# Attention scores on row halves, normalisation moved to the routing phase, value products of two steps together

## The reference

```python
x = L0_attn_x                       # (4, 2048, 256), float32
xn = _layernorm(x, axis=-1)
x = x + _L0_attn_ref(xn, ...) + _L0_ffn_ref(xn, ...)
# inside _L0_ffn_ref:
h = _rmsnorm(xn, g1)
q = (h @ Wq).reshape(B, S, 16, 16); c = h @ Wdkv
k = (c @ Wuk).reshape(B, S, 16, 16); v = (c @ Wuv).reshape(B, S, 16, 16)
scores = where(causal, einsum("bqhd,bkhd->bhqk", q, k) / sqrt(16), -1e9)
out = einsum("bhqk,bkhd->bqhd", softmax(scores, axis=-1), v).reshape(B, S, D)
x2 = xn + out @ Wo
x2 = x2 + _moe(_rmsnorm(x2, g2), gate_w, w1, w2)   # 8 experts, 2 per token
```

## Time and profile before

| | us |
|---|---|
| runs of the kernel before (3) | 3376.55, 3378.97, 3382.85; median 3378.97 |
| the profiled execution, its own time | 3397.75 |
| its span in the profile | 3396.2 |
| PE, DVE, ACT, POOL busy in it | 2743.9, 2474.5, 1561.3, 2210.9 |
| phase 1 / phase 2 / phase 3 | 0 to 467 / 467 to 2277 / 2285 to 2570 |

### The profile page before, as it was taken

One profiled execution on the slowest core, in us unless ns is written; L12 is line 12 of the kernel. 1 busy time (PEld: TensorE's weight loads), 2 busy tenths in 40 slices (PEclk: granted clock), 3 DMA queues, 4 the chain that ended last, 5 costly groups with the idle time before them and its releaser, 6 DMA issues. The chain is left out here.

```text
span 3396.2 us, 56592 instructions
## 1 busy us (share of the span) xinstructions
PE 2743.9 (81%) x16988; PEld 1397.0 (41%) x17168; DVE 2474.5 (73%) x3932; ACT 1561.3 (46%) x2346; POOL 2210.9 (65%) x1179
## 2 busy tenths in 40 slices
PE   5959978998989898989899989977766988889700
PEld 2535532333333323332333333226655777777600
DVE  5538868877878797889778887714444999999444
ACT  2312235565656665666556666662222444444200
POOL 3423359678767966796669777964663666666476
PEclk9979999999999999999999999997767999999855
DMA  4995560443144214422442240016546666666676
GB/s 135 215 287 194 190 151 18 62 62 54 31 63 64 45 39 63 64 41 44 62 62 36 47 64 14 19 33 222 193 143 214 215 210 199 210 201 206 216 219 208
DMA packets 366323, 408.79 MB, mean 120 GB/s; under 512 B 66690, under 2 KB 310788, under 8 KB 366084
## 3 DMA queue, kind: packets, MB, share of 16 engines
q1 hardware_dynamic: 320132, 323.96, 39.2%
q0 software_dynamic: 17920, 54.55, 5.0%
q10 hardware_dynamic: 28032, 27.27, 2.3%
HBM read 256.12 MB, written 149.03 MB: 119 GB/s over the span
## 5 line engine op out<-in xcount | busy, mean ns | idle before, releaser
L885 DVE TENSOR_REDUCE p_piece_max<-p_ring 128x1 f32<-128x512 f32 (+3 forms) x2160 | 1319.0, 656 | 189.1 <-PE p_ring L1010 94.5
L959 ACT ACTIVATE p_probs<-p_st 128x1024 f32<-128x1024 f32 (+3 forms) x1280 | 1078.0, 894 | 682.5 <-PE p_st L1045 342.4
L827 POOL TENSOR_TENSOR p_terms<-p_head_p,p_head_in 128x4096 f32<-128x4096 f32 x32 | 347.7, 10865 | 314.4 <-ACT p_head_p L966 313.7
L1042 PE MATMUL p_st<-unit_q,unit_k 98*128 98x512 bf16 (+7 forms) x1642 | 433.7, 353 | 51.5 <-DMA unit_q<-p_neg_lo 31.5
L1057 PE MATMUL p_pv<-p_probs,unit_vg 128*32 128x512 f32 (+3 forms) x3520 | 409.6, 542 | 0.0
L1687 POOL TENSOR_TENSOR p_pv<-p_pr,p_qkv 128x4096 f32<-128x4096 f32 x32 | 347.8, 10868 | 38.6 <-ACT p_pr L1785 37.9
L1004 PE MATMUL p_ring<-unit_k,unit_q 64*128 64x512 bf16 (+3 forms) x1600 | 275.2, 358 | 75.0 <-DVE p_piece_max L885 74.5
L1858 PE MATMUL p_y_ps<-p_w,p_hid 128*128 128x256 f32 x1152 | 281.0, 400 | 31.6 <-ACT p_hid L1798 31.6
L812 POOL TENSOR_TENSOR p_terms<-p_head_in 128x4096 f32<-128x4096 f32 x32 | 282.0, 8814 | 4.9 <-POOL p_head_s L820 4.4
L1845 PE MATMUL p_hid_ps<-p_rT,p_w 128*128 128x256 f32 x1152 | 263.9, 382 | 4.8 <-issue 4.3
L833 POOL TENSOR_TENSOR p_terms<-p_terms 128x2048 f32<-128x2048 f32 (+2 forms) x96 | 252.6, 2632 | 17.1 <-POOL p_terms L833 11.4
(11 more groups left out here) (202 smaller groups left out, 3825.4 us busy)
## 6 DMA issues: line engine op xcount, KB each, us to landing
p_w<-ffn_w SPq DMA_DIRECT2D x144, 512.0 KB, 5.2
qk_parts<-p_parts SPq DMA_DIRECT2D x64, 384.0 KB, 3.3
head_qkv<-p_heads SPq DMA_DIRECT2D x16, 1536.0 KB, 6.2
p_rows<-sorted_rows SPq DMA_DIRECT2D x72, 256.0 KB, 4.5
expert_rows<-p_y ACTq DMA_DIRECT2D x72, 256.0 KB, 5.8
unit_q<-qk_parts SPq DMA_DIRECT2D x132, 128.0 KB, 10.3
unit_k<-qk_parts SPq DMA_DIRECT2D x132, 128.0 KB, 10.8
p_x<-attn_x SPq DMA_DIRECT2D x32, 512.0 KB, 5.2
```

What stands on the lines that cost most here:

```text
L827: step(nc.gpsimd.tensor_tensor(terms[:, :, :, :], head_p[:, u, :, :].unsqueeze(2).to_broadcast([P, H, DH, H]), head_in[:, u, 2, :, :].rear ...
L885: nc.vector.tensor_reduce(piece_max[:, h:h + heads, i, pc], ring_ps[bank][:, 0:heads * width].rearrange("p (h k) -> p h k", h=heads), AX_X ...
L959: nc.scalar.activation(probs[:, 2 * turn_of(s, i) + u, :, 0:width], st_ps[u][:, :, 0:width], ACT.Exp).then_inc(probs_done, 1)
L1042: last = nc.tensor.matmul(st_ps[u][:, j, 0:width], k6[s][0:rows, hh, kt * P:(kt + 1) * P], q6[s][0:rows, hh, c * CT + skip:(c + 1) * CT], ...
```

## The change

1. **Row halves.** The six parts of two heads stand in rows 0 to 63 and those of the other two in rows 64 to 127; parts 4 and 5 and the maxima stand in a second pair of slots, 34 rows long. A score is now two passes, of 64 and of 34 rows, each a pair of matmuls on the two halves of the array. A mask is 64 columns on one half. `score_pair` and, in phase 1, `row_piece` use the same halves.
2. **Division.** `turn` and `divide` go. The values with their sums are stored as they stand (17 rows of 512, four DMAs for each c) in a DRAM tensor `o_with_sums`. For each unit SP gathers the sums of the unit before right behind its last store, DVE inverts them at step 10 (`invert_sums`), and SP stores the inverses. Phase 3 loads the values already turned, with the inverses broadcast over 16 rows each, and multiplies on DVE; `transpose_o` and `copy_oT` go.
3. **Order.** LAG is 3 with 8 buffers of probabilities in place of 6. Even steps: scores, maxima, scores, maxima. Odd steps: scores, scores, maxima, the values of two steps, maxima.
4. **Ones.** Rows of ones are written by DMAs (8 behind the loads in phase 1, 4 at the start of phase 2); the memsets of `set_constant_rows` go, zeros are not needed.
5. `head_max` has two buffers.

```diff
@@ constants and helpers
+HALF = 4 * DH
+PASS_ROWS = (HALF, NEG + 2)
+SUMS = DH + 1
...
+def gather_sums(eng, sums, sums_of, n, loaded):
+    for hh in range(HG):
+        eng.dma_start(sums[hh * VW:(hh + 1) * VW, :], sums_of[n, hh, DH, :].rearrange("(q j) -> q j", q=VW)).then_inc(loaded, 16)
...
+def add_mask(nc, out, half, j, mask, ident_b):
+    rows = slice(half * HALF, (half + 1) * HALF)
+    return nc.tensor.matmul(out[:, j * HALF:(j + 1) * HALF], mask[rows, j + 1 - half, :], ident_b[rows, rows],
+                            start=False, stop=True, skip_group_check=True)
@@ phase2_attend, SP
+            def store_o(n, c):
+                wait_apart(sp, pv_copied, NC * n + c + 1, apart)
+                for hh in range(HG):
+                    sp.dma_start(sums_of[n, hh, :, c * CT:(c + 1) * CT],
+                                 pv_sb[hh * VW:hh * VW + SUMS, c % 2, :]).then_inc(o_stored[c % 2], 16)
+
+            def load_sums(n):
+                for slot in range(2):
+                    wait_apart(sp, o_stored[slot], N_STORE_O * (1 + NC // 2 * (n + 1)), apart)
+                wait_apart(sp, inverse_done, n + 1, apart)
+                gather_sums(sp, sums, sums_of, n, sums_loaded)
...
+                if n + 2 < UNITS:
                     wait_apart(sp, pv_done, LAG + 1 + N_STEP * n, apart)
                     load(sp, n + 2, (s + 2) % SLOTS)
                 if n:
-                    store_o(n - 1, NC - 1, ring_item(n, s, 0)[0])
+                    store_o(n - 1, NC - 1)
+                    load_sums(n - 1)
+                store_o(n, 0)
+                if n:
+                    store_inverse(n - 1)
@@ phase2_attend, DVE
+            def invert_sums(n):
+                dve.wait_ge(sums_loaded, N_STORE_O * (n + 1))
+                dve.wait_ge(inverse_stored, 16 * (n + 1))
+                nc.vector.reciprocal(inverse[:, :], sums[:, :]).then_inc(inverse_done, 1)
...
-                    if i in TURN_AT:
-                        c = TURN_AT.index(i)
-                        divide(n, c, *ring_item(n, s, turn_item(c, has_next)))
+                    if i == INVERSE_AT and not first(n):
+                        invert_sums(n - 1)
@@ phase2_attend, PE, scores
-                rows = SCORE_ROWS[u]
-                for j in range(2):
-                    hh = 2 * u + j
-                    last = nc.tensor.matmul(st_ps[u][:, j, 0:width], k6[s][0:rows, hh, kt * P:(kt + 1) * P],
-                                            q6[s][0:rows, hh, c * CT + skip:(c + 1) * CT], start=True, stop=not diagonal)
+                for second in range(2):
+                    for half in range(2):
+                        rows = half_rows(half, second)
+                        last = nc.tensor.matmul(st_ps[u][:, half, 0:width], k6[s][rows, PAIR * second + u, kt * P:(kt + 1) * P],
+                                                q6[s][rows, PAIR * second + u, c * CT + skip:(c + 1) * CT], start=second == 0,
+                                                stop=second == 1 and not diagonal, skip_group_check=True)
@@ phase2_attend, PE, steps
-                    scores(n, s, i, 0)
-                    scores(n, s, i, 1)
-                    if i == 0 and not first(n):
-                        turn(n - 1, NC - 1, *ring_item(n, s, 0))
-                    maxima(done, cut)
-                    if i >= LAG:
-                        values(n, s, i - LAG)
+                    scores(n, s, i, 0)
+                    if i % 2 == 0:
+                        maxima(done, cut)
+                        scores(n, s, i, 1)
+                    else:
+                        scores(n, s, i, 1)
+                        maxima(done, cut)
+                        if i >= LAG:
+                            values(n, s, i - LAG)
+                            values(n, s, i - LAG + 1)
                     maxima(cut, upto)
@@ phase3_route, SP, load
-                sp.dma_start(o[:, c, :, :], o_v[b, c]).then_inc(loaded[c], 16)
+                for g in range(NG):
+                    k, rows = g // UNITS_K, slice(g % UNITS_K * HG * DH, (g % UNITS_K + 1) * HG * DH)
+                    sp.dma_start(oT[rows, c, k, :], o_v[b, c, g, :, 0:DH, :]).then_inc(loaded[c], 16)
+                for k in range(KD):
+                    sp.dma_start(inverse[:, c, k, :], inverse_v[b, c, k].unsqueeze(1).to_broadcast([UNITS_K * HG, DH, CT])).then_inc(loaded[c], 16)
@@ phase3_route, DVE
+            def divide(b, c):
+                dve.wait_ge(loaded[c], N_LOADED * (b + 1))
+                nc.vector.tensor_tensor(oT[:, c, :, :], oT[:, c, :, :], inverse[:, c, :, :], ALU.mult).then_inc(divided, 1)
```

More of the change, by code:

```diff
@@ L73, in store_neg, with set_ones @@
 def store_neg(sp, q6, neg_hi, neg_lo, stored):
-    for half, hs in enumerate(HALVES):
+    for half in range(2):
         for r, part in enumerate((neg_hi, neg_lo)):
-            row = NEG_ROW[half] + r
-            sp.dma_start(q6[row:row + 1, hs, :].rearrange("a h (i p) -> a (h i) p", p=P),
+            row = half * HALF + NEG + r
+            sp.dma_start(q6[row:row + 1, PAIR:HG, :].rearrange("a h (i p) -> a (h i) p", p=P),
                          part[half * PAIR * KT:(half + 1) * PAIR * KT, :]).then_inc(stored, 16)
[L81 to L89, removed]
+def set_ones(eng, k6, ones, stored):
+    for half in range(2):
+        row = half * HALF + NEG
+        for slot in range(PAIR, HG):
+            eng.dma_start(k6[row:row + 2, slot, :].rearrange("r (c t) -> r c t", c=NC),
+                          ones[0:2, :].unsqueeze(1).to_broadcast([2, NC, CT])).then_inc(stored, 16)
@@ L98, in row_piece @@
-    if diagonal:
-        last = nc.tensor.matmul(out[:, width - P:width], ident_b[:, :], mask_q[:, :], start=False, stop=True)
+    half, slot = h // PAIR, h % PAIR
+    rows = half_rows(half, 0)
+    last = nc.tensor.matmul(out[:, 0:width], q6[rows, slot, i * P:(i + 1) * P], k6[rows, slot, pc * CT:pc * CT + width],
+                            start=True, stop=pc != i // TT, skip_group_check=True)
+    if pc == i // TT:
+        for j in range(2):
+            last = add_mask(nc, out[:, width - P:width], half, j, mask_q, ident_b)
@@ L283, in _ @@
             load_unit(sp, qk_heads, v_units, 1, *units[1], next_loaded)
+            for _, k6_u, _ in units:
+                set_ones(sp, k6_u, ones, next_loaded)
             with sp.Fori(1, B - 1) as b:
@@ L757, in _ @@
             sp.sem_inc(neg_stored, 64)
-            def body(n, s, loads, has_next):
-                if loads:
+            wait_apart(sp, consts, 1, apart)
+            set_ones(sp, k6[2], ones, ones_set)
+            for n in range(UNITS):
+                s = n % SLOTS
+                if n + 2 < UNITS:
                     wait_apart(sp, pv_done, LAG + 1 + N_STEP * n, apart)
@@ L1163, in phase3_route @@
         table_i = sb("p3_table_i", [P, 2, N_TILE], mybir.dt.int32)
-        oT_ps = [bank(f"p3_oT{k}_ps") for k in range(KD)]
         mla_ps = [bank(f"p3_mla{i}_ps") for i in range(2)]
@@ L1351, in _ @@
             for c in range(2):
+                divide(0, c)
+            for c in range(2):
                 add_attention(0, c, c)
```

254 lines of the change are left out of this document (108 added, 146 removed).

## The result

The changed kernel takes 3552.28 us (median of 4 runs, 3548.29 to 3556.96) against 3380.91 (4 runs of the kernel before, 3376.55 to 3392.16): ratio 1.0502, 95% interval 1.0472 to 1.0532. It is 5% slower; forecast was 3548. The profiled execution took 3556.96 with a span of 3555.1, 158.9 us more than the span before.

What follows compares the result with a forecast made beforehand. PE and DVE, coupled through a short ring, bound the kernel; 146 − 14 − 3 + 11 + 4 + 0 + 25 = +169 on the profiled 3397.75 gave 3567, or 3548 against the median; range 3372 to 3605.

Steps and rivals of the forecast that it cites:

- The wait at step 10: Phase 2: DVE waits for the gathered sums of the unit before, until 40.0 us after the first score.
- The choice: Last stores of a unit: 17-row transfers run on one engine (5.8 to 6.8 us), not spread over 16 (0.4 us).
- DVE's arrival: Phase 2 units: DVE reaches step 10 at 27.5 us after the unit's first score.
- The rest of a unit: Phase 2, step 10 to the next unit's first score: 84.0 us, plus 1.5 for half clock after PE's stand.
- rival (d): Phase 2: DVE does not starve at the values, but the wait is long; 3457 us, chance 0.10.
- (a): Stores and turned loads spread over all engines, units wait only till 34.7 us; 3426 us, chance 0.17.
- (b): Phase 2: the wait at step 10 does not happen; 3319 us, chance 0.16 with its mixed case.
- (e): PE: the halves of a score do not run side by side; far above 3700 us, chance 0.01.
- rival (c): Phase 2: PE stays at half clock for a further 10 us after standing; 3593 us, chance 0.09.
- Unit 0: First unit of phase 2: POOL's memsets, behind which scores and `shift_heads` wait, go; 14 us less.
- Phase 1: Earlier start without memsets −16, DMAs of ones +3, changes of matmul shape +13; sum 0.
- Phase 3: Transposes go (−29), start +7, but unevenly cut loads make the loop bound by DMA; +25 us with the start.

Runs made afterwards that it cites:

- even_again: Changed kernel with inversion at step 16, values of one step at a time, and values and sums stored apart in even row counts: 3307.16 us, 0.9792 of kernel before.
- single_again: Changed kernel with inversion at step 16 and values of one step at a time, uneven loads kept, same chip: 3331.28 us, 0.9848 of kernel before.

## Why the prediction was right

**The wait at step 10** happened as forecast: the reciprocal at 38.1 us after the first score in the mean (38.4 at the middle) for 39.7 (40.0 less 0.3). It is the term that decided, and both ways of taking it off confirm it. The 68 runs took 5.5 us on one engine, where the sum had 0.4 + 5.3 = 5.7 and its long end 5.8 to 6.8: the price of a run, 0.1 us, was read off phase 3 and is 0.08 here. The stores begin 29.0 us after the first score for 29.95, and from their end to the reciprocal it is 3.5 us for 4.1. **The choice** between the two ends was right: 17 rows went over one engine (share 0.07), and 20 rows over about ten (80 runs in 1.5 us, 10 or 11 at a time, for c > 0). What its reason says of the even counts is in the traces as well: loads of 16 rows (q and k) have up to 17 to 19 runs at a time and a share of 1.05, stores of 32 rows up to 16 to 18, loads of 64 up to 18 (even_again), and those of 128 (v) up to 27, with a share of 0.95. That the divisors of a count decide was the author's estimate, with which 17 and 20 agree.

**DVE's arrival** was off: 29.9 us (38.1 less 8.2 of wait in each of 13 units) for 27.5, so that the wait was 8.2 where the sum implied 12.2. The step that failed is the sum before step 10: it had no stand of PE at step 7. In the five units whose step 7 took its plain 4.4 to 4.7 us DVE arrives at 28.0, in the eight others (6.7 to 9.7) at 31.2. In the change the wait swallowed the stand, so the total did not notice; with the wait gone it came out.

**The rest of a unit** is 124.6 − 38.1 = 86.5 for 85.5. The block of two whole steps took 5.86 for 5.71, DVE's starving 0.86 for 0.83, so rival (d) falls; (a) and (b) fall with the wait. In the change the halves of a score start 3 to 4 ns apart for the most part and its two passes 0.21 to 0.23 us, so they do run side by side and (e) falls. The 0.21 for 512 columns is 0.22 from start to start in the trace before (L1042), and the 0.86 is twice the 0.43 to 0.45 between the two records of a values matmul. The clock fell to 0.50 behind the wait, as the 1.5 assumed, for some 6 us of PE's work and not the 10 of rival (c). Steps 10 and 11 take 9.4 us longer in units 1 to 13 than with the inversion at step 16, 1.2 more than the wait; no run shows the clock's part of this by itself.

**Unit 0** gained 7 for 14, and by another way than forecast. What stretches step 12 there (10.4 us for 2.6) is DVE's subtraction in `shift_heads`. It starts 1.3 us into an operation of POOL and ends 0.3 us behind its end; in the change it meets a shorter one of POOL (the kernel before, then the change):

```profile
504.07 8.77 POOL L812 TENSOR_TENSOR p_terms<-p_head_in 128x4096 f32<-128x4096 f32 x1 [0.28 <-POOL p_head_s L820]
505.32 7.80 DVE L920 TENSOR_TENSOR p_head_s<-p_head_s,p_head_max 128x256 f32<-128x256 f32 x1
```

```profile
497.76 4.49 POOL L851 TENSOR_TENSOR p_terms<-p_terms 128x2048 f32<-128x2048 f32 x1 [0.18 <-POOL p_terms L846]
499.04 3.50 DVE L948 TENSOR_TENSOR p_head_s<-p_head_s,p_head_max 128x256 f32<-128x256 f32 x1
```

In units where POOL stands still it takes 0.42 us. So 4.3 of the 7 us are this: the memsets (14 us of POOL) mattered by which operation of POOL they put beside it, though no run moved POOL alone. The term was read off POOL's busy time and should have been read off DVE's row. **Phase 1** gained 4 where I had 0. **Phase 3** came out at 26 for 25, by the forecast's parts only in sum: the start lost 14 where 7 and a share of the DMA's term were meant, the chunks 12, at 16.0 us each ((2705.7 − 2465.9)/15) where 17 or more was the sign. That the cut of the loads is a good part of it is shown by even_again: 23 us. On how many engines the cut loads went, four or eight in the forecast, no run shows exactly; at most 6 of their runs lie over each other, and 9 with the inverses (single_again).

**How near it came** is in part luck. On the profiled executions the forecast was 3567 and the measured time 3556.96: units 1 to 13 cost 13 us less than forecast, phase 1 4 less, and unit 0 gained 7 less. The medians agree within 4 us because the execution profiled before lay 18.8 above its median and the one profiled after only 4.7.

## What to carry to other kernels

Count the rows of a transfer before its bytes: four transfers with 17 rows each ran on one DMA engine (5.5 us), and with 20 or 32 rows, and more bytes, they were faster (2.5 us at most). A wait inserted into an engine that is coupled to the others by a short ring can cost its full length on all of them (here 8.2 us of wait and 8.5 us of a unit); put results that are long in coming behind work that is needed anyway, or their stores ahead of a burst of loads in the same queue. When work is grouped to save changes of shape, look at the largest distance it leaves between two deliveries to the engine that sets the pace.

## What the runs showed of the hardware that was not expected

PE stood up to 7.1 us with no releaser in a burst of 4 MB of loads, in kernels with 21392 matmuls, and not when the same loads came in six portions; nor did it in the kernel before, with the same burst and 16988. The packets show blocks of 16 KB on an instruction queue, and each of the 37 stands ended 1.3 to 2.0 us behind the end of one. With the loads in portions the kernel took 40 us less as a whole.

Two chips differed by 1.5% in the time of the kernel before, and by 20 us in the chunks of phase 3 of the same kernel (even loads, 201.9 and 221.9), though with the uneven loads all three chips took 234 to 241: the gain of a stage is only to be had from runs on one chip, and need not be the same on the next.
